# Search rounds of a vision tower's router: counts by masks and folded products, keys made per half

## The reference

```python
input_acts = gelu(einsum('bsd,nd->bsn', x, input_patterns))      # (64, 196, 2048)
input_acts_seq = input_acts.mean(axis=1)                          # (64, 2048)
top_input_acts, top_input_idx = top_k(input_acts_seq, 256)        # of 2048
input_repr = zeros((B, 2048)).at[brow, top_input_idx].set(top_input_acts)
process_acts = gelu(einsum('bn,pn->bp', input_repr, process_input_weights))   # (64, 1024)
top_process_acts, top_process_idx = top_k(process_acts, 128)
aggregated_value = einsum('bk,bkd->bd', softmax(top_process_acts), process_values[top_process_idx])
output_acts_seq = gelu(einsum('bd,od->bo', aggregated_value, output_input_weights))   # (64, 2048)
top_output_acts, top_output_idx = top_k(output_acts_seq, 256)     # of 2048
out_per_seq = einsum('bk,bkm->bm', top_output_acts, output_patterns[top_output_idx])
output = broadcast_to(out_per_seq[:, None, :], (B, S, 256))       # added to every token
```

## Time and profile before

| what | us |
|---|---|
| median of 3 runs | 1622.32 (1618.98 to 1623.66) |
| the profiled execution | 1622.39 |
| its span in the profile | 1620.6 |
| tower, to 1394.7 | 1394.7 |
| first stage's two searches, 1399.7 to 1451.6 | 51.9 |
| second stage's two searches, 1518.7 to 1571.1 | 52.4 |
| output, 1585.9 to 1620.6 | 34.7 |

### The profile page before, as it was taken

One profiled execution on the slowest core, in us unless ns is written; L12 is line 12 of the kernel. 1 busy time (PEld: TensorE's weight loads), 2 busy tenths in 40 slices (PEclk: granted clock), 3 DMA queues, 4 the chain that ended last, 5 costly groups with the idle time before them and its releaser, 6 DMA issues. The chain is left out here.

```text
span 1620.6 us, 31966 instructions
## 1 busy us (share of the span) xinstructions
PE 1477.4 (91%) x9800; PEld 1384.3 (85%) x9800; DVE 965.0 (60%) x2416; ACT 948.0 (58%) x3363; POOL 120.8 (7%) x247
## 2 busy tenths in 40 slices
PE   7899999999999999999999999999999999774431
PEld 6799999999999999999999999999999998771330
DVE  5756665555555555555555555565566643485686
ACT  4566666666666666666666666666666655771440
POOL 1000000000000000000000000000000000000000
PEclk9999999999999999999999999999999999757555
DMA  9311111111111111111111111111110000267007
GB/s 207 78 45 46 45 44 44 44 44 40 40 42 44 44 44 44 44 44 44 41 40 40 39 40 39 40 39 44 44 44 10 10 11 11 105 215 297 0 0 317
DMA packets 53237, 99.36 MB, mean 61 GB/s; under 512 B 16720, under 2 KB 35664, under 8 KB 52176
## 3 DMA queue, kind: packets, MB, share of 16 engines
q1 hardware_dynamic: 52272, 98.22, 20.7%
q10 hardware_dynamic: 928, 0.69, 0.2%
HBM read 73.17 MB, written 25.69 MB: 61 GB/s over the span
## 5 line engine op out<-in xcount | busy, mean ns | idle before, releaser
L669 ACT ACTIVATE ffn<-ffn 128x196 f32<-128x196 f32 x1024 | 328.8, 321 | 208.6 <-PE ffn L545 208.2
L545 PE MATMUL ffn<-x_t_hi,pat_w_hi 128*128 128x392 f32 x1024 | 361.4, 353 | 1.4 <-DVE x_t_lo L824 1.4
L545 PE MATMUL ffn<-x_t_lo,pat_w_hi 128*128 128x392 f32 x1024 | 348.3, 340 | 0.0
L545 PE MATMUL ffn<-x_t_hi,pat_w_lo 128*128 128x392 f32 x1024 | 348.2, 340 | 0.0
L760 DVE SCALAR_TENSOR_TENSOR shared<-shared,gen 98x512 f32<-98x512 f32 x64 | 44.1, 689 | 276.6 <-ACT shared L642 276.6
L545 PEld LDWEIGHTS ffn<-x_t_hi,pat_w_hi 128*128 128x128 f32 x1024 | 192.9, 188 | 5.7 <-DVE x_t_lo L824 1.6
L545 PEld LDWEIGHTS ffn<-x_t_lo,pat_w_hi 128*128 128x128 f32 x1024 | 194.2, 190 | 1.2
L669 ACT ACTIVATION_READ_ACCUMULATOR ffn<-ffn 128x1 f32 x1024 | 193.2, 189 | 0.0
L545 PEld LDWEIGHTS ffn<-x_t_hi,pat_w_lo 128*128 128x128 f32 x1024 | 192.8, 188 | 0.0
L473 PE MATMUL gen<-qkvu_w_lo,h_t_hi 128*98 128x512 f32 (+1 forms) x512 | 173.0, 338 | 0.0
L473 PE MATMUL gen<-qkvu_w_hi,h_t_hi 128*98 128x512 f32 (+1 forms) x512 | 172.9, 338 | 0.0
(11 more groups left out here) (228 smaller groups left out, 2798.4 us busy)
## 6 DMA issues: line engine op xcount, KB each, us to landing
raw<-in_x_dram SPq DMA_DIRECT2D x752, 56.0 KB, 2.0
h_dram<-h SPq DMA_DIRECT2D x128, 98.0 KB
process_nat<-ocess_input_weights_dram SPq DMA_DIRECT2D x8, 1024.0 KB, 4.8
process_t<-h_dram SPq DMA_DIRECT2D x8, 896.0 KB, 11.0
out_dram<-process_t SPq DMA_DIRECT2D x8, 896.0 KB, 6.2
h_early<-h_dram SPq DMA_DIRECT2D x4, 896.0 KB, 12.4
out_dram<-h_early SPq DMA_DIRECT2D x3, 896.0 KB, 4.5
pat_nat<-_ffn_input_patterns_dram SPq DMA_DIRECT2D x1, 2048.0 KB, 9.4
```

The lines of the kernel that those rows point to most:

```text
L545: last = pe.matmul(fb[f % FFN_BANKS][:, 0:T2], a[:, d, f * P:(f + 1) * P], b[:, d, :], start=n == 0, stop=n == 3 * s.halves - 1)
L669: last = act.activation(cols, cols, ACT.Gelu, accum_out=gelu_sum[:, par, at:at + 1])
```

## The change

In every round VectorE's two counting instructions become five comparisons without a tally. They write masks of ones and zeros: both candidates now for all 1024 words, in pieces of 512 and 512, and of 512, 256 and 256. TensorE does the counting: it multiplies each block of 64 mask columns by the matrix that adds an image's two partitions, 32 products that all add into 2 x 64 columns of PSUM; the group is opened by a product of zeros over 192 columns. ScalarE counts for the third candidate alone; its tally enters as one column of a 64-column operand, just ahead of the last four mask products. VectorE then reduces the 3 x 64 sums to three (a new instruction with a wait of its own) before it judges them. One PSUM bank holds the tally where two took turns. In the second stage five fillers follow each round; 24 fillers are put ahead of the ranks' transposes. The keys are made in two halves of 512, each as soon as ScalarE has written that half of `wide`. The table of steps loses the half step that only ScalarE's share of the second candidate needed.

```diff
-        SHARED_AT = 5 * HALF // 8
-        reached_too = sb("reached_too", [P, 2 * HALF - SHARED_AT], BF16)
+        BLOCK = 64
+        reached_too = sb("reached_too", [P, HALF], BF16)
+        HALF_CUTS = [0, HALF // 2, HALF]
+        LAST_CUTS = [0, HALF // 2, 3 * HALF // 4, HALF]
+        masked_pieces = [(m, slice(a, b)) for m, cuts in enumerate((HALF_CUTS, LAST_CUTS)) for a, b in zip(cuts, cuts[1:])]
+        MASKS = len(masked_pieces)
...
+        signs = sb("signs", [P, BLOCK], F32R)
+        counts = sb("counts", [P, 3])
+        zeros = sb("zeros", [P, 3 * BLOCK], BF16)
+        image_sum = sb("image_sum", [P, P], BF16)
...
-        tallies = [sums, turn[2]]
+        tally = turn[2]
...
             def sum_halves(n):
-                tally = tallies[n % 2][:, 0:4]
                 if n == 0:
                     pe.wait_ge(numbers_made, 1)
-                if n >= 2:
-                    pe.wait_ge(judged, n - 1)
-                pe.matmul(tally, image_sum[:], offset, start=True, stop=False)
-                pe.wait_ge(counted_too, n + 1)
-                pe.matmul(tally, image_minus_half[:], signs, start=False, stop=False)
-                pe.wait_ge(counted, n + 1)
-                pe.matmul(tally, image_sum[:], count, start=False, stop=True).then_inc(summed, 1)
+                if n >= 1:
+                    pe.wait_ge(counted, n)
+                pe.matmul(tally[:, 0:3 * BLOCK], image_sum[:], zeros[:], start=True, stop=False)
+                for piece, (m, cols) in enumerate(masked_pieces):
+                    if piece == MASKS - 1:
+                        pe.wait_ge(counted_too, n + 1)
+                        pe.matmul(tally[:, 2 * BLOCK:3 * BLOCK], image_minus_half[:], signs[:], start=False, stop=False)
+                    pe.wait_ge(masked, MASKS * n + piece + 1)
+                    for at in range(cols.start, cols.stop, BLOCK):
+                        last = pe.matmul(tally[:, m * BLOCK:(m + 1) * BLOCK], image_sum[:], reached[m][:, at:at + BLOCK],
+                                         start=False, stop=piece == MASKS - 1 and at + BLOCK == cols.stop)
+                last.then_inc(summed, 1)
...
+            pe.wait_ge(copied, fills + out_fills)
+            pe.wait_ge(taken, 2 * (s.k_proc // 8 - 6))
+            keep_busy(24)
             pe.wait_ge(ranks_found, 1)
...
             for n in range(STAGE, 2 * STAGE):
                 sum_halves(n)
-            pe.wait_ge(wide_made, 2)
+                keep_busy(5)
+            pe.wait_ge(wide_made, 4)
             keep_busy(6)
...
-                    act.activation(reached_too[:, 0:HALF], word[:], ACT.Sign, scale=-1.0, bias=tried[:, 4:5],
-                                   accum_out=signs[:, 2:3])
-                    act.activation(reached_too[:, HALF:], word[:, SHARED_AT:], ACT.Sign, scale=-1.0,
-                                   bias=tried[:, 3:4], accum_out=signs[:, 1:2]).then_inc(counted_too, 1)
+                    act.activation(reached_too[:], word[:], ACT.Sign, scale=-1.0, bias=tried[:, 4:5],
+                                   accum_out=signs[:, 0:1]).then_inc(counted_too, 1)
...
-                        for m, cols in enumerate((HALF, SHARED_AT)):
-                            last = dve.tensor_scalar(reached[m][:, 0:cols], word[:, 0:cols], tried[:, 1 + m:2 + m],
-                                                     0.0, ALU.is_ge, ALU.add, accum_out=count[:, m:m + 1])
-                        last.then_inc(counted, 1)
+                    for m, cols in masked_pieces:
+                        dve.tensor_scalar(reached[m][:, cols], word[:, cols], tried[:, 1 + m:2 + m], None,
+                                          ALU.is_ge).then_inc(masked, 1)
...
                     dve.wait_ge(summed, n + 1)
-                    dve.tensor_scalar(passed[:], tallies[n % 2][:, 0:3], float(s.k_in), 0.0, ALU.is_ge, ALU.add,
+                    dve.reduce_sum(counts[:], tally[:, 0:3 * BLOCK].rearrange("p (m b) -> p m b", b=BLOCK),
+                                   axis=AX.X).then_inc(counted, 1)
+                    dve.wait_ge(counted, n + 1)
+                    dve.tensor_scalar(passed[:], counts[:], float(s.k_in), 0.0, ALU.is_ge, ALU.add,
                                       accum_out=found[:]).then_inc(judged, 1)
...
-                after(tie_step, dve.tensor_copy(word[:], words[:, :, 1]))
+                for n in range(2):
+                    cols = slice(n * 512, (n + 1) * 512)
+                    dve.wait_ge(wide_made, 2 * stage - 1 + n)
+                    after(tie_step, dve.tensor_scalar(mask[:, cols], bits[:, cols], 31, 0x7FFFFFFF,
+                                                      ALU.arith_shift_right, ALU.bitwise_and))
+                    dve.scalar_tensor_tensor(key[:, cols], mask[:, cols], 0x8000, bits[:, cols],
+                                             ALU.bitwise_xor, ALU.bitwise_xor).then_inc(keys_made, 1)
+                    dve.wait_ge(keys_made, 2 * stage - 1 + n)
+                    after(tie_step, dve.tensor_copy(word[:, cols], words[:, cols, 1]))
```

More of the change, by code:

```diff
@@ L994, in route @@
         ahead = sb("ahead", [P, 5])
[L995 to L998, removed]
+        blank = sb("blank", [P, BLOCK])
+        signs = sb("signs", [P, BLOCK], F32R)
+        counts = sb("counts", [P, 3])
+        zeros = sb("zeros", [P, 3 * BLOCK], BF16)
+        image_sum = sb("image_sum", [P, P], BF16)
         image_minus_half = sb("image_minus_half", [P, P], F32R)
@@ L1018, in route @@
         acts_turned, wide_made, chosen = sem("acts_turned"), sem("wide_made"), sem("chosen")
-        words_made, tried_made, numbers_made, counted, counted_too = sem("words_made"), sem("tried_made"), sem("numbers_made"), sem("counted"), sem("counted_too")
+        words_made, tried_made, numbers_made, counted, counted_too, masked = sem("words_made"), sem("tried_made"), sem("numbers_made"), sem("counted"), sem("counted_too"), sem("masked")
         summed, ahead_made, judged = sem("summed"), sem("ahead_made"), sem("judged")
@@ L1090, in _ @@
             pool.wait_ge(masks_made, 5)
-            pool.memset(blank[:, 9:10], (HALF - SHARED_AT) / 2)
-            pool.memset(blank[:, 10:11], HALF / 2).then_inc(masks_made, 1)
+            pool.memset(blank[:, 1:2], float(-HALF)).then_inc(masks_made, 1)
             pool.tensor_tensor(tie_share[:], other_half[:], same_image[:], ALU.subtract).then_inc(masks_made, 1)
@@ L1190, in _ @@
             pe.transpose(turn[1][:, 0:s.k_proc], ranked_t[:], w.ident[0:s.k_proc, 0:s.k_proc]).then_inc(ranks_turned, 1)
-            pe.wait_ge(copied, fills + out_fills)
             keep_busy(5)
@@ L1238, in _ @@
                 act.wait_ge(acts_turned, n + 1)
-                last = act.activation(wide[:, n * 512:(n + 1) * 512], turn[n][:], ACT.Copy, scale=1.0 / s.tokens)
-            last.then_inc(wide_made, 1)
+                act.activation(wide[:, n * 512:(n + 1) * 512], turn[n][:], ACT.Copy,
+                               scale=1.0 / s.tokens).then_inc(wide_made, 1)
             def count_too(n, search):
@@ L1248, in count_too @@
                 with nc.allow_low_precision(reason="whole numbers up to 1024"):
-                    act.activation(reached_too[:, 0:HALF], word[:], ACT.Sign, scale=-1.0, bias=tried[:, 4:5],
-                                   accum_out=signs[:, 2:3])
-                    act.activation(reached_too[:, HALF:], word[:, SHARED_AT:], ACT.Sign, scale=-1.0,
-                                   bias=tried[:, 3:4], accum_out=signs[:, 1:2]).then_inc(counted_too, 1)
+                    act.activation(reached_too[:], word[:], ACT.Sign, scale=-1.0, bias=tried[:, 4:5],
+                                   accum_out=signs[:, 0:1]).then_inc(counted_too, 1)
             def keep_low_words(stage):
-                act.wait_ge(keys_made, stage)
+                act.wait_ge(keys_made, 2 * stage)
                 act.activation(low_word[:], sure[:].bitcast(I16).rearrange("p (n w) -> p n w", w=2)[:, :, 0],
@@ L1281, in _ @@
             act.activation(tie_signs[:], blank[:, 0:2], ACT.Copy)
-            act.activation(numbers[:], blank[:], ACT.Copy).then_inc(numbers_made, 1)
+            act.activation(zeros[:], same_image[:, 0:1].to_broadcast([P, 3 * BLOCK]), ACT.Copy, scale=0.0)
+            act.activation(signs[:], blank[:], ACT.Copy).then_inc(numbers_made, 1)
             act.activation(both_halves[:], same_image[:, 0:B].unsqueeze(2).to_broadcast([P, B, 2]), ACT.Copy)
@@ L1318, in _ @@
                 act.wait_ge(output_product, n + 1)
-                last = act.activation(wide[:, n * 512:(n + 1) * 512], prod[n][:], ACT.Gelu, scale=total[:])
-            last.then_inc(wide_made, 1)
+                act.activation(wide[:, n * 512:(n + 1) * 512], prod[n][:], ACT.Gelu,
+                               scale=total[:]).then_inc(wide_made, 1)
             for search in (2, 3):
@@ L1347, in try_three @@
                     n, at = search * ROUNDS + r, 6 * r
-                    if n == 0:
```

(18 more changed lines are left out.)

## The result

The changed kernel takes 1616.09 us (median of 6 runs, 1612.79 to 1620.21) against 1622.88 of the kernel before (6 runs, 1618.98 to 1625.24): ratio 0.9963, 95% interval 0.995 to 0.9975, 4 to 8 us less. The forecast was 1615.2. The profiled execution takes 1616.47 us, its span is 1614.7.

A forecast was written before the change was run, and what follows sets the result against it. It took the searches' chain of waits, counting shared by VectorE and ScalarE, as the bound. Raised-clock rounds -10.6, first rounds +3.3, fillers +0.6, keys -0.5: -7.2 us from 1622.39, forecast 1615.2 us, its own range 1610 to 1619.

The forecast's parts named there:

- The round at the raised clock: One search round with TensorE at its upper clock: 2.71 us, 0.38 less than now, for 28 of 32 rounds.
- signs of being wrong: Last four products of a round waiting for earlier ones instead of the last mask, or clock 0.50 through the rounds.
- Masks: VectorE's comparisons without tally in each round: 0.269 ns a word, half of the slow end.
- rival B: No change: masks in the rounds run at the slow end, 0.538 ns a word; 1627 us, chance 0.14.
- Product spacing: TensorE's 64-column mask products in a round follow each other by 0.031 us at the raised clock, keeping up with masks.
- rival A: Slower: weight loads set the spacing of the mask products in the rounds; 1644 us, chance 0.14.
- the first round of each search at the lower clock and the other 28 at the upper: Clock assumed in the four searches: four first rounds of 3.91 us, 0.82 more than now each, +3.3 us.
- the fillers: Fillers behind the first round in the last two searches delay the next: 0.3 us for each search, +0.6.
- Keys: Keys made per half ahead of the searches start earlier: 0.5 us gained for both stages together.
- Rival C: Slower: the clock never rises in the rounds, which take 4.4 or 4.9 us; 1672 us, chance 0.07.
- Rival D: Faster still: the clock also stays up through the stages between, -5 us; 1610 us, chance 0.13.

The follow-up runs named there:

- e4_block128: The changed kernel with mask blocks of 128 columns instead of 64, so 14 + 2 products a round and a reduction over 384 sums: 1620.52 us.
- e2_ahead: The changed kernel with 16, 13, 12 and 12 fillers (products nobody reads) ahead of the first round of searches 1 to 4: 1610.01 us.
- e5_no24: The changed kernel without the 24 fillers ahead of the transposes of the ranks: 1618.18 us.
- e7_steps: The changed kernel with VectorE's wait for the steps' transfer moved from ahead of the first keys to behind them: 1616.05 us.
- e3_nofill: The changed kernel without the five fillers behind each round of searches 3 and 4: 1625.09 us.
- e8_all_warm: The changed kernel with fillers in every TensorE pause behind the tower, and the wait for the steps behind the first keys: 1602.48 us.
- e1_keys: The kernel before with the keys made per half and nothing else of the change: 1620.21 us.
- e6_before_warm: The kernel before, rounds unchanged, with 10 and 12 fillers ahead of searches 3 and 4 and nine behind each of their rounds: 1619.64 us.

## Why the prediction was right, and which term was mis-sized

- **The round at the raised clock: right.** Forecast 2.71 us, measured 2.685. Last mask's end 1.27 us after the start (1.28), last four products at 1.43 (1.41 to 1.50), reduction begun at 1.76 (1.77), itself 0.36 (0.35). One of my signs of being wrong, last products that wait for earlier ones, did appear: they start 0.16 us after the last mask's end, where a mask that is waited for has its first product 0.05 us after its end. But the sum had them behind the product of the signs, so the sign was drawn wrongly, not the term.
- **Masks: right.** (350 - 281) / 256 = 0.27 ns a word, half of the slow end; rival B is out. The Trainium skill, page VectorE: DVE Perf Modes (Mode 4×_2P), with an estimate of 0.26 ns a word, agrees.
- **Product spacing: right.** 0.029 us at the raised clock against my 0.031 from L487, and below the 0.045 at which rival A would have decided. In e4_block128 products of 128 columns, each with its own load, follow each other by 0.056 us.
- **The step that was mis-sized: "the first round of each search at the lower clock and the other 28 at the upper".** It is two rounds. The first took 3.50 us, less than my 3.91, because the products at the lower clock follow each other by 0.053 us and not by 0.062 (in the timeline of the first round the first of the 28 starts at 1398.11 and the last at 1399.54) and the last one takes 0.24 us and not 0.37. The second took 3.49, 3.87, 3.60 and 4.11, since the clock rose only within it and its zeros stood behind transposes or fillers at the lower clock. Against 2.685 the first rounds cost 4 x 0.82 = 3.3 us (forecast 4.8), the second ones 4.3 (forecast 0.6, for the fillers). The searches gained 98.84 - 93.81 = 5.0 us instead of 6.7. e2_ahead, which takes the pause away and gets 7.2 us back, shows where they went. The number of slow rounds varies: search 2 had one in e5_no24 and e7_steps (22.28 us), two in the changed kernel.
- **Keys: the sum right, its parts not.** Forecast -0.5 for both. Measured +0.6 ahead of search 1, where the keys begin with the steps' transfer and not with ScalarE, as the chain above shows and e7_steps confirms, and -1.0 ahead of search 3: -0.4.
- **Rival C nearly came true.** The rounds alone do not raise the clock (e3_nofill). Its price, 4.4 to 4.9 us a round with transposes or fillers, no run shows: the 3.50 us of e3_nofill is a round without either.
- **Rival D did not happen.** L1209 after (L1199 before) is 3.67 us as in the earlier trace rows, L1219 3.69 against 3.15, L1235 6.08 against 5.37. e8_all_warm shows that what it looked for is there: with 2.0, 1.9 and 3.7 us the three lose 4.6 of their time in the earlier trace rows, about the 5 that I had put.
- **The time: close to the forecast, in part by chance.** Searches (5.0), keys (0.4) and the ranks' transposes (0.3, e5_no24) give 5.7 us where I had 7.2; the medians differ by 6.8, the interval is 4 to 8, and against the 27 and 20 later runs of the kernel before (1622.23 and 1622.29) the gain is 6.1 to 6.2. The two profiles show what scatters around these terms. Behind the tower they differ by 3.4 us only (225.9 to 222.6). The tower, which the change leaves alone, gave 2.6 more: the first transpose behind it starts between 1391.6 and 1396.0 in the ten profiles. The three groups of products L1161, L1209 and L1224, which it leaves alone as well, took 2.6 us back, and there it is the clock. L1161 took 13.95 us in the profile of before, at 1.00 from its first product on; in e1_keys, whose instructions there are the same, it began at 0.50 and took 15.72, and in the changed kernel 15.31. Its first stretch in before, and in e1_keys:

```profile
1460.13:1462.00 1.87, 1.87 (x11) 0.73 (x12) 0.00 (x0) 0.60 (x1) 0.00 (x0) 1.00 0.97 403
1462.30:1464.00 1.70, 1.70 (x5) 0.54 (x6) 0.00 (x0) 0.60 (x1) 0.00 (x0) 0.50 1.02 422
```

## What to carry to other kernels

Before the change TensorE was busy for 37.5 of 51.9 us in the first searches and yet ran at half its clock; nothing in the busy shares said so. Read the granted clock of each stage, and cost a step that moves work to TensorE at both clocks before choosing one. Products that nobody reads, written in the pause ahead of a dependent chain and sized to end just before it, were worth more here (13.6 us, on top of the changed kernel and with the edit of e7_steps) than the rewriting of the chain (6.8 us), and the rewriting without those behind the rounds of searches 3 and 4 was a loss (e3_nofill). What they would give in the kernel before is shown for searches 3 and 4 alone (e6_before_warm); no run fills all its pauses. Where a piece is started earlier, look for the next wait in front of it: here it was a transfer of constants that started as the first transpose did (1392.05 and 1392.08).

## What the runs showed that I had not expected

- The granted clock still reads 0.97 in the 3.0 us without products between searches 1 and 2, and 0.50 in the 3.7 us from the next search's start; with 13 fillers in that pause it reads 1.00 on both sides.
- The fall of the clock does not come at a fixed time behind a pause. In e4_block128 the clock still read 1.00 in the pause ahead of search 2, the first round took 2.91 us like a fast one, and the second 3.70:

```profile
1424.40:1427.40 3.00, 0.00 (x0) 0.00 (x0) 2.86 (x5) 0.00 (x0) 0.00 (x0) 1.00 0.72 216
1427.40:1430.40 3.00, 2.51 (x26) 2.35 (x26) 2.42 (x12) 2.23 (x5) 0.00 (x0) 0.84 0.34 139
```

- One round of the fourth search, its seventh, takes 0.35 us more than its neighbours (3.03 against 2.68) in every kernel with folded rounds, also at the raised clock (3.03 in e8_all_warm), and in none with the old ones. VectorE stands idle there between L1367 and L1372; no run here says why.
